# A third context buffer and regrouped tap operands, reordered small loads, and up-projection weights made one stage earlier

## The chip, the cores and the metric

The kernel runs on one core of one Trainium2 chip. The metric is the device time of one launch in microseconds (us), taken as the median of three runs. Below, PE is TensorE, DVE is VectorE, ACT is ScalarE, POOL is GpSimd, and SP is SyncE, which here only issues DMAs.

## The reference, cut to what matters

One decoder layer in fp32, batch 4, 1024 positions, width 512. Three sublayers, each followed by a layer norm: windowed self-attention, a cross-attention block with an S4D convolution and its own feed-forward part, and a second feed-forward part made of butterfly matrices. The parts that the change touches:

```python
K = 2.0 * jnp.einsum('dn,dnl->dl', dC, powers).real   # taps, (512, 1024)
K_ = (x_vision @ Wk)                                   # context keys, 4 x 2048 rows of 384
...
y = jnp.fft.irfft(xf * Kf.T[None], n=n, axis=1)[:, :L]
xt = x_text + y * (1 + gate * scale_out) + gate * shift_out
h = layernorm(xt, g_ffn, b_ffn)
h = gelu(h @ W1 + b1) @ W2 + b2                        # W1 (512, 2048)
xt = layernorm(xt + h, g_norm_out, b_norm_out)
...
h = butterfly(x @ W_exp + b_exp, up_weights, 2048)     # folded into w3, b3 by the kernel
h = butterfly(gelu(h + up_bias), down_weights, 2048)   # folded into w4
```

## The kernel before, in words

The kernel is a row of stages, each with its own on-chip buffers and semaphores. Between two stages all engines meet: DMAs have landed, POOL clears the semaphores of the stage, and then the next stage starts on every engine. So time saved or lost in a stage counts in full, and what the trace shows as idle at the start of a stage is on the path. Inside a stage every engine has its own list of instructions in the order in which the code is written, with waits on semaphores. There is no scheduler.

**Taps stage** (`stage_taps`, buffers `tp_`, 0 to 298 us). First the attention weights are folded (PE, ACT, to 72 us). Then four rounds, one for each 128 channels `c`: `turn(c, 0)` transposes the first power table in 32 PE transposes that ACT copies out in 8 (line 400); `key_groups(c)` loads four blocks of 512 context rows (`context`, line 201, on SP), transposes them and projects them on the key weights; `turn(c, 1)` does with the second table what `turn(c, 0)` did; `taps(c)` multiplies the tables (line 264, 32 fp32 matmuls of 128x128, which the trace records as 64), and ACT copies each group of four out of PSUM in four pieces of 32x128 into `krow` (line 409). Meanwhile DVE computes the tables of the next round (`first_table`, `second_table`). SP waits for `krow`, stores it, reads it back turned as `kd`, and only then comes to the context loads of the next round. There are two context buffers. The copy of the second table writes single floats 128 bytes apart, since `tabT[1]` is stored channel by channel; the matmul at line 264 reads its moving operand in single floats 512 bytes apart.

**Folding stage** (`stage_butterfly`, `bf_`, 298 to 437 us). SP loads `low_up` (2 MB), the bias of the expansion as a column of single floats, and `col_up` (four loads, 4096 runs of 16 bytes in all); ACT at the same time loads 8 MB of weights in rows of 8 and 4 KB. DVE multiplies out the low butterfly steps from `low_up` into `e_up` (line 844). PE then needs `e_up`, the bias and `col_up` all together for its bias product (line 747), from which the rest of the stage follows. At the end the result `w3` is stored by SP (line 701) and the bias `b3` by ACT (line 819), again as single floats.

**Inverse stage** (`stage_idft`, `id_`, 2732 to 2965 us). Four batches of four tiles; a tile is 96 matmuls of 128x512 on PE, some 12 us, then ACT and DVE form sum and difference, PE reverses the difference with an exchange matrix, ACT copies it to `rev` (two buffers) and POOL stores both.

**Feed-forward stage** (`stage_mlps`, `m_`, 2965 us to the end). Sixteen groups of 512 positions, for each 16 chunks of hidden units: `up` (12 matmuls into `ps_h`), Gelu on ACT (line 3006), split into high and low part on DVE (line 3138) and POOL, `down` (12 matmuls into `ps_o`). Every fp32 product is made of three fp32r products of high and low parts (`mm3`, lines 80 to 82). Before the first group the stage loads W1 in four slabs, scales it with `g_ffn` into high and low part (`up_hi` on ACT, `up_lo` on DVE), and adds `b_ffn @ W1` to the bias: `bias_products(s)`, 16 matmuls of one column, which the trace records as 32 (line 2873). One of these blocks stands ahead of the first transposes and three inside the first group. All of this waits for seven small loads, four of which are columns of single floats:

```python
up_slab(0)
for t, v in ((bf, ...b_ffn), (gf, ...g_ffn), (b1[:, 0, :], ...b1), (b1[:, 1, :], b3)):
    sp.dma_start(t[:, :], column(v), ...).then_inc(s_c, 16)      # 2730
for t, v in ((b2, ...), (g_row, ...), (b_row, ...)):
    sp.dma_start(t[:, :], row(v)).then_inc(s_c, 16)              # 2732
...
pe.wait_ge(s_c, 16 * 7)
bias_products(0)
for q in range(Q):
    turn(0, 0, q)
up(0, 0, 0, 0)
bias_products(1)
```

The order of the first four tiles there is fixed by the code too: POOL does `modulate(q + 1)` before `power(q)`, and ACT issues the loads of tile 3 only after the copy `hi` of tile 0.

## Time and profile before

| | us |
|---|---|
| median of three runs (lowest, highest) | 4554.81 (4554.34, 4557.46) |
| the profiled execution's own time | 4548.83 |
| its span in the trace | 4547.2 |
| taps stage (from the timeline) | 0 to 297.8 |
| folding stage | 297.8 to 437.2 |
| inverse stage | 2732.1 to 2964.7 |
| feed-forward stage | 2964.7 to the end |
| mean granted clock of TensorE, share of full speed | 0.944 |

The busy share of PE over the whole span is 87%. This is an average: in the stages between 437 and 2732 us nothing is changed, and the four stages of the table each have stretches in which PE stands still. The timeline of one engine has a bracket behind a row with the idle time before it and what ended it; the windows view gives busy time, granted clock and DMA share of a stretch.

### The profile page before, as it was taken

The numbers are of one execution on the slowest core, as the hardware profiler recorded it, in microseconds if no ns is written. First come the engines' busy times: TensorE is split into PE (matmuls) and PEld (weight loads), VectorE is DVE, ScalarE is ACT, GpSimd is POOL, SyncE is SP. The second block draws the span as 40 slices with busy tenths as digits, with TensorE's granted clock in tenths as the row PEclk, the third lists the DMA queues.
The fourth block names the chain that finished last, engine by engine and source line by source line (L and its number), as shares of the span: only waits on it lengthen the run. The fifth ranks groups of instructions, "written<-read, shape, count | busy, mean of one in ns | idle before, by whom it ended". The sixth has DMA issues, their size and how long they took to land. (4 is left out here: it accounts for less than half of the span.)

```text
span 4547.2 us, 61734 instructions
## 1 busy us (share of the span) xinstructions
PE 3933.9 (87%) x20188; PEld 3234.0 (71%) x20188; DVE 2528.2 (56%) x8674; ACT 1507.1 (33%) x2415; POOL 2027.3 (45%) x1411
## 2 busy tenths in 40 slices
PE   7856999958668888887899997959999999999998
PEld 4642778747668777786787775748877877778786
DVE  8815676578888888884555553224433445222222
ACT  3644454346546666664101002211111112111111
POOL 0000111157567787776564240036766765323332
PEclk9978999969889999998999998969999999999999
DMA  3454423220100111000542223341212232000000
GB/s 104 135 165 110 130 86 106 86 71 12 50 25 12 50 33 50 29 12 21 210 142 102 97 103 141 116 146 59 70 59 66 71 96 67 19 22 28 23 23 19
DMA packets 244938, 337.06 MB, mean 74 GB/s; under 512 B 66898, under 2 KB 125170, under 8 KB 241268
## 3 DMA queue, kind: packets, MB, share of 16 engines
q1 hardware_dynamic: 154868, 186.17, 13.5%
q10 hardware_dynamic: 87184, 138.46, 8.9%
q0 software_dynamic: 2560, 8.39, 0.5%
q8 instruction: 167, 2.74, 0.2%
q14 instruction: 159, 1.30, 0.1%
HBM read 220.70 MB, written 112.25 MB: 73 GB/s over the span
## 5 line engine op out<-in xcount | busy, mean ns | idle before, releaser
L2832 POOL TENSOR_TENSOR m_act_hl<-m_g,m_act_hl 128x512 fp32r<-128x512 f32 x256 | 355.3, 1388 | 681.0 <-DVE m_act_hl L3138 680.9
L1624 PE MATMUL xa_ps_t<-xa_diag,xa_s_buf 128*128 128x128 f32 x4096 | 520.6, 288 | 141.8 <-ACT xa_a L1711 74.8
L1624 PEld LDWEIGHTS xa_ps_t<-xa_diag,xa_s_buf 128*128 128x128 f32 x4096 | 507.7, 202 | 163.3 <-issue 81.0
L3138 DVE CAST m_act_hl<-m_g 128x512 fp32r<-128x512 f32 x256 | 139.6, 545 | 852.1 <-ACT m_g L3006 851.8
L1788 DVE MAX8 xa_cand<-xa_s_buf 128x8 f32<-128x64 f32 x4096 | 542.5, 218 | 63.3 <-ACT xa_s_buf L1674 37.4
L3006 ACT ACTIVATE m_g<-m_ps_h,m_b 128x512 f32<-128x512 f32 x256 | 176.1, 688 | 1117.7 <-PE m_ps_h L82 1112.6
L80 PE MATMUL m_ps_h<-m_hT,m_w 128*128 128x512 f32 x1024 | 417.7, 408 | 19.8 <-issue 17.7
L82 PE MATMUL m_ps_h<-m_hT,m_w 128*128 128x512 f32 x1024 | 409.8, 400 | 0.0
L81 PE MATMUL m_ps_h<-m_hT,m_w 128*128 128x512 f32 x1024 | 409.7, 400 | 0.0
L80 PE MATMUL m_ps_o<-m_w,m_act_hl 128*128 128x512 f32 x1024 | 407.1, 398 | 0.7 <-POOL m_act_hl L2832 0.7
L82 PE MATMUL m_ps_o<-m_w,m_act_hl 128*128 128x512 f32 x1024 | 406.9, 397 | 0.0
L81 PE MATMUL m_ps_o<-m_w,m_act_hl 128*128 128x512 f32 x1024 | 406.9, 397 | 0.0
L1552 POOL TENSOR_SCALAR xa_s_buf<-xa_s_buf,xa_top 128x1024 f32<-128x1024 f32 x120 | 342.9, 2858 | 141.4 <-ACT xa_prob L1693 141.4
L1554 POOL TENSOR_TENSOR xa_s_buf<-xa_s_buf,xa_prob 128x1024 f32<-128x1024 f32 x120 | 318.3, 2652 | 18.0 <-issue 0.4
L1674 ACT ACTIVATE xa_s_buf<-xa_ps_s 128x2048 f32<-128x2048 f32 x128 | 239.4, 1870 | 140.5 <-PE xa_ps_t L1624 75.4
L1693 ACT ACTIVATE xa_prob<-xa_s_buf,xa_nmax 128x2048 f32<-128x2048 f32 x128 | 252.6, 1998 | 88.0 <-POOL xa_s_buf L1554 88.0
L1591 PE MATMUL xa_ps_s<-xa_ks,xa_qs 128*128 128x512 f32 x512 | 159.2, 435 | 123.2 <-ACT xa_s_buf L1674 108.6
L80 PEld LDWEIGHTS m_ps_h<-m_hT,m_w 128*128 128x128 f32 x1024 | 195.7, 191 | 69.9 <-issue 24.8
L82 PEld LDWEIGHTS m_ps_h<-m_hT,m_w 128*128 128x128 f32 x1024 | 195.7, 191 | 47.4
L80 PEld LDWEIGHTS m_ps_o<-m_w,m_act_hl 128*128 128x128 f32 x1024 | 193.5, 189 | 48.7 <-POOL m_act_hl L2832 2.0
L81 PEld LDWEIGHTS m_ps_h<-m_hT,m_w 128*128 128x128 f32 x1024 | 196.4, 192 | 43.8
L82 PEld LDWEIGHTS m_ps_o<-m_w,m_act_hl 128*128 128x128 f32 x1024 | 193.8, 189 | 46.9
(384 smaller groups left out, 8329.6 us busy)
## 6 DMA issues: line engine op xcount, KB each, us to landing
at_xk<-in_x_dram SPq DMA_DIRECT2D x128, 128.0 KB, 2.8
spectrum<-df_yo ACTq DMA_DIRECT2D x32, 512.0 KB, 2.8
id_raw<-spectrum SPq DMA_DIRECT2D x32, 512.0 KB, 5.6
m_xt<-x ACTq DMA_DIRECT2D x64, 256.0 KB, 3.8
tp_awT<-in_ctx_dram SPq DMA_DIRECT2D x16, 768.0 KB, 4.6
xa_ks<-kt SPq DMA_DIRECT2D x48, 256.0 KB
xa_raw<-in_ctx_dram SPq DMA_DIRECT2D x32, 384.0 KB, 3.4
kt<-tp_aw SPq DMA_DIRECT2D x4, 2048.0 KB, 6.6
```

The costliest lines, as they stand in the source:

```text
L80: pe.matmul(out, w_hi, m_lo, start=start, stop=False)
L81: pe.matmul(out, w_lo, m_hi, start=False, stop=False)
L82: return pe.matmul(out, w_hi, m_hi, start=False, stop=stop)
L1552: pool.tensor_scalar(half, half, top[:, t % 2, h, TOPK - 1:TOPK], None, ALU.is_ge)
L1554: pool.tensor_tensor(half, half, prob[:, h % 2, HALF:S2], ALU.mult).then_inc(s_psel, 1)
L1591: last = pe.matmul(ps_s[:, c, :], qs[:, t % 2, h, :], ks[:, h, c * 512:(c + 1) * 512], start=True, stop=True)
L1624: last = pe.matmul(ps_t[:, c // 4, c % 4, :], s_buf[:, t % 2, h, k0:k0 + P], diag[:, h, :], start=(h == 0 and c % 4 == 0), stop=(h == HEAD ...
L1674: act.activation(s_buf[:, t % 2, h, :], ps_s[:, :, :].rearrange("p c n -> p (c n)"), ACT.Copy).then_inc(s_sc, 1)
L1693: act.activation(prob[:, h % 2, :], s_buf[:, t % 2, h, :], ACT.Exp, bias=nmax[:, t % 2, h:h + 1], scale=SCALE).then_inc(s_exp, 1)
L1788: dve.max(out=ranks[h][:, :, g], in_=s_buf[:, t % 2, h, :].rearrange("p (n g e) -> p g n e", g=SEGS, e=4)[:, g, :, :])
L2832: pool.tensor_tensor(lo, g32[:, :], hi.bitcast(F32), ALU.subtract).then_inc(s_gl, 1)
L3006: act.activation(g32[:, :], ps_h[:, n % 2, :], ACT.Gelu, bias=b1[:, cur, n:n + 1]).then_inc(s_g, 1)
```

## The change

Taps: a third context buffer (in a part of `aw` that the folding results use until they are stored, so SP waits for these stores before it loads the third block), context loads one block further ahead; the matmul at line 264 takes its columns in the order (r, d), so that it reads runs of four floats; `ps_k` has that order too; the copy of the second table writes runs of four floats and reads PSUM with a stride of 512 bytes; the copies to `krow` read PSUM with a stride of 16 bytes.

Folding: the bias and `col_up` are loaded ahead of `low_up`; biases come as ready [128, 16] tables, which the host lays out; `b3` is stored by rows, ahead of the `out_t` copies.

Inverse and feed-forward stage: W1's buffers become shared by both (`UpTiles`). The four slabs and the small columns (as ready tables) are loaded during batches 0 and 1; in batch 2 each tile is followed by one bias block on PE, four scalings on ACT and five instructions on DVE. `rev` has one buffer in place of two, and its copy waits until both stores of the tile before have landed. The inverse stage has eight semaphores more, the feed-forward stage two fewer.

```diff
@@ stage_taps @@
-        ps_k = psum("ps_k", [P, 2, 4, 4, R])
+        ps_k = psum("ps_k", [P, 2, 4, R, 4])
+        third = aw[:, 0, :, :].rearrange("p e n -> p (e n)")
+        raw = [... for r in (turned[:, 0:4 * DV], turned[:, 4 * DV:2 * 4 * DV], third[:, 0:4 * DV])]
...
-                    if g >= 2:
-                        sp.wait_ge(s_ct, VC * (g - 1))
+                    if g >= 3:
+                        sp.wait_ge(s_ct, VC * (g - 2))
...
                 context(1)
+                sp.wait_ge(s_fs[0], 16 * (DC + 2))
+                sp.wait_ge(s_fs[1], 16 * (DC + 1))
+                context(2)
...
-                                             tabT[0][:, :, d].rearrange("p r d -> p d r"), start=True, stop=True)
+                                             tabT[0][:, :, d], start=True, stop=True)
...
+                            out = tabT[1][...].rearrange("p (d r) -> p d r", r=R)
+                            act.activation(out[:, :, 4 * g:4 * g + 4], ps_t[:, n % 2, :, :].rearrange("p q d -> p d q"), ACT.Copy)
...
+                        products = ps_k[:, g % 2].rearrange("p q a d -> p q d a")
-                            last = act.activation(channels[:, :, d, :], ps_k[R * d:R * (d + 1), g % 2, :, d, :], ACT.Copy)
+                            last = act.activation(channels[:, :, d, :], products[R * d:R * (d + 1), :, d, :], ACT.Copy)
@@ stage_butterfly @@
-                sp.dma_start(low_up[:, 0:LOW_LEN], A["butterfly_up"]).then_inc(s_lu, 16)
-                sp.dma_start(wT[:, :, D:D + 1], A["L0_ffn_b_exp"].rearrange(...), allow_slow_non_contiguous=True)
+                sp.dma_start(bias[:, :], A["L0_ffn_b_exp_columns"]).then_inc(s_cup, 16)
                 for k in range(TOP):
                     sp.dma_start(col_up[:, k, :, :], ...).then_inc(s_cup, 16)
+                sp.dma_start(low_up[:, 0:LOW_LEN], A["butterfly_up"]).then_inc(s_lu, 16)
...
+                act.wait_ge(s_hi, 1)
+                act.dma_start(b3_out, upb[:, :]).then_inc(s_b3, 16)
                 for n in range(0, 16, 2):
...
-                act.dma_start(b3_out.rearrange("(c p) -> p c", p=P), upb[:, :], allow_slow_non_contiguous=True)
@@ stage_idft @@
-        rev = sb("rev", [P, 2, D])
+        rev = sb("rev", [P, D])
...
+                        if b == UPB:          # PE, after reverse(n - 1); UPB = 2
+                            bias_products(t)
...
+                def bias_products(s):
+                    pe.wait_ge(s_w1[s], 16)
...
+                    for n in range(4 * s, 4 * s + 4):
+                        for c in range(DC):
+                            last = pe.matmul(ps_b[:, n:n + 1], upt.raw1[:, c, n * P:(n + 1) * P], upt.bf[:, c:c + 1], ...)
...
-                    act.wait_ge(s_st[k], 32 * stores)
+                    if n >= 1:
+                        act.wait_ge(s_st[1 - k], 32 * ((n - 1) // 2 + 1))
@@ stage_mlps @@
-                up_slab(0)
-                for t, v in ((bf, ...), (gf, ...), (b1[:, 0, :], ...), (b1[:, 1, :], b3)):
-                    sp.dma_start(t[:, :], column(v), allow_slow_non_contiguous=True).then_inc(s_c, 16)
...
                 sp.wait_ge(s_mod, 2)
-                up_slab(1)
-                sp.wait_ge(s_mod, 3)
-                up_slab(2)
-                up_slab(3)
...
-                pe.wait_ge(s_c, 16 * 7)
-                bias_products(0)
```

The SP list of the folding stage, before:

```order
L686 DMA bf_low_up<-in_butterfly_up_dram 128x4064
L687 DMA bf_wT<-in_L_ffn_b_exp_dram 128x16x1
L689 DMA bf_col_up<-in_L_ffn_up_weights_dram 128x8x4 x4
L690 DMA bf_wv<-in_L_xattn_Wv_dram 128x3x512
L691 DMA bf_gate<-in_L_xattn_mod_gate_dram 128x1
```

and after:

```order
L694 DMA bf_bias<-in_L_ffn_b_exp_columns_dram 128x16
L696 DMA bf_col_up<-in_L_ffn_up_weights_dram 128x8x4 x4
L697 DMA bf_low_up<-in_butterfly_up_dram 128x4064
L698 DMA bf_wv<-in_L_xattn_Wv_dram 128x3x512
L699 DMA bf_gate<-in_L_xattn_mod_gate_dram 128x1
```

The 2 MB of `low_up` now stand behind the small pieces on the same queue.

The PE list where the inverse stage ends (`id_`) and the feed-forward stage (`m_`) begins, before:

```order
L2484 MATMUL id_ps_rev<-id_out,id_flip 128x512 x2
L2443 UNCONDITIONAL_BRANCH
L2853 UNCONDITIONAL_BRANCH
L2873 MATMUL m_ps_o<-m_bf,m_raw_33048 128x1 x16
L2861 MATMUL m_ps_t<-m_ident,m_h 128x128 x16
L80 MATMUL m_ps_h<-m_hT,m_w 128x512
```

and after:

```order
L2521 MATMUL id_ps_rev<-id_out,id_flip 128x512 x2
L2473 UNCONDITIONAL_BRANCH
L2902 UNCONDITIONAL_BRANCH
L2910 MATMUL m_ps_t<-m_ident,m_h 128x128 x16
L80 MATMUL m_ps_h<-m_hT,up_w 128x512
```

The block of 16 one-column matmuls is gone there. It now stands, four times, in batch 2 of the inverse stage, each time between the reversal and the next tile:

```order
L82 MATMUL id_ps<-id_y,id_mats 128x512
L2521 MATMUL id_ps_rev<-id_out,id_flip 128x512
L2555 MATMUL id_ps_b<-up_bf,up_raw_31619 128x1 x16
L80 MATMUL id_ps<-id_y,id_mats 128x512
L81 MATMUL id_ps<-id_y,id_mats 128x512
```

The four blocks, one ahead of the first transposes and three inside the first group, have moved between the tiles of batch 2.

## Rows read from the trace of the kernel before

**Rows 1.** The page: busy time and share of the span of each engine.

```profile
PE 3933.9 (87%) x20188; PEld 3234.0 (71%) x20188; DVE 2528.2 (56%) x8674; ACT 1507.1 (33%) x2415; POOL 2027.3 (45%) x1411
```

**Rows 2.** Groups by line and shape, whole span: busy, mean ns | idle before.

```profile
L1104 PE MATMUL at_ps_t<-at_xT,at_m_qk 128*128 128x128 f32 x1024 | 126.6, 278 | 2.4 <-ACTq L1187 2.4
...
L264 PE MATMUL tp_ps_k<-tp_tabT 128*128 128x128 f32 x256 | 57.0, 397 | 4.5 <-ACT tp_tabT L400 4.5
...
L409 ACT ACTIVATE tp_krow<-tp_ps_k 32x128 f32<-32x128 f32 x128 | 34.4, 269 | 27.4 <-PE tp_ps_k L264 26.3
```

**Rows 3.** The tile `tabT`: shortest, median and longest ns of its copies.

```profile
L400 ACT ACTIVATE tp_tabT<-tp_ps_t x64: 591/816/1147, 72.0 to 262.7; 128x512 f32<-128x512 f32 x64
```

**Rows 4.** Timeline of ACT, last round: start, duration, what, idle before.

```profile
256.33 7.36 ACT L400 ACTIVATE tp_tabT<-tp_ps_t 128x512 f32<-128x512 f32 x8
...
278.03 1.11 ACT L409 ACTIVATE tp_krow<-tp_ps_k 32x128 f32<-32x128 f32 x4 [0.64 <-PE tp_ps_k L264]
```

**Rows 5.** Timeline of PE: round 1 begins; last of three context waits.

```profile
123.03 1.06 PE L253 MATMUL tp_ps_t<-tp_ident,tp_tab 128*128 128x128 f32 x8
...
241.64 1.09 PE L282 MATMUL tp_ps_w<-tp_ident,tp_awT 128*128 128x128 f32 x8 [1.45 <-DMA tp_awT<-in_ctx_dram]
```

**Rows 6.** Timeline of DVE: the instruction behind the first table of round 1.

```profile
118.83 2.29 DVE L535 TENSOR_TENSOR tp_aw<-tp_aw 128x2048 fp32r<-128x2048 f32 x1 [0.17 <-issue]
```

**Rows 7.** DMA queues, 312 to 316 us: packets, MB, share of 16 engines.

```profile
q10 hardware_dynamic: 280, 1.56, 96.0%
q1 hardware_dynamic: 281, 0.00, 4.2%
```

**Rows 8.** DMA queues, 325 to 326 us.

```profile
q1 hardware_dynamic: 1508, 0.02, 85.1%
```

**Rows 9.** Timeline, folding stage: `low_up` is there, `e_up` ends, the bias product.

```profile
308.22 0.29 DVE L844 TENSOR_TENSOR bf_half<-bf_low_up 128x32 f32<-128x32 f32 x2 [49.45 <-DMA bf_low_up<-in_butterfly_up_dram]
...
311.81 2.36 DVE L844 TENSOR_TENSOR bf_e_up<-bf_half,bf_low_up 128x1024 f32<-128x1024 f32 x2
...
329.59 6.96 PE L747 MATMUL bf_ps_b<-bf_wT,bf_e_up 128*128 128x1 f32 x32 [9.25 <-issue]
```

**Rows 10.** Timeline: first instruction of the stage after folding.

```profile
437.23 0.20 POOL L1035 MEMSET at_ident<- 128x128 f32 x1 [138.78 <-POOLq L66]
```

**Rows 11.** Tile `b` (the store of `b3`): issue to landing.

```profile
DMA to landing us min/median/max: 14.3/14.3/14.3
```

**Rows 12.** Tile `bf_out_t` (16 stores of `w3`): issue to landing.

```profile
DMA to landing us min/median/max: 2.4/2.9/13.5
```

**Rows 13.** Timeline, end of the inverse stage and start of the next.

```profile
2956.81 0.54 POOL L2474 DMA_DIRECT2D conv<-id_rev  x1 [0.64 <-ACT id_rev L2524]
2964.65 0.37 SPq L2719 DMA_DIRECT2D m_raw<-in_L_xattn_W_dram  x1
```

**Rows 14.** The chain that ended last, feed-forward stage: start, us, what.

```profile
2981.55 13.75 issue
...
3000.83 6.20 issue
3007.03 1.30 POOLq L2795
...
3018.11 0.80 PE m_ps_h L80
```

**Rows 15.** Timeline of PE, first group: the second of four bias blocks.

```profile
3022.93 4.24 PE L2873 MATMUL m_ps_t<-m_bf,m_raw 128*128 128x1 f32 x32
```

**Rows 16.** Timeline of ACT: first and fifth Gelu of the first group.

```profile
3023.13 0.69 ACT L3006 ACTIVATE m_g<-m_ps_h,m_b 128x512 f32<-128x512 f32 x1 [4.50 <-PE m_ps_h L82]
...
3061.22 0.69 ACT L3006 ACTIVATE m_g<-m_ps_h,m_b 128x512 f32<-128x512 f32 x1 [3.16 <-PE m_ps_h L82]
```

**Rows 17.** Windows: PE, PEld, DVE, ACT, POOL busy; granted clock; DMA share; GB/s.

```profile
3027.20:3032.30 5.10, 5.10 (x13) 3.95 (x14) 2.10 (x4) 0.00 (x0) 0.00 (x0) 0.50 0.00 0
...
2809.00:2857.00 48.00, 47.04 (x197) 36.41 (x196) 15.78 (x18) 13.79 (x18) 4.32 (x8) 1.00 0.35 127
```

205 lines of the change are left out of this document (96 added, 109 removed).

## The prediction

> **What bounds the kernel now.** I read the page first. TensorE is busy for 87% of the span [rows 1], but that is a mean over stages, and the stages meet at barriers, so I went stage by stage: the timelines of the engines in the four stages that change, the chain of waits at the start of the feed-forward stage, the DMA queues where loads compete, and the windows for the clock. The reader is to see four things. In the taps stage PE and ACT take turns on the path: a strided copy of tables lasts 7.4 us for eight [rows 4], a plain one is half as long [rows 3], and ACT waits 26 us for the tap matmuls [rows 2]. In the folding stage PE waits until 329.6 us for small loads, though `e_up` was ready at 311.81 + 2.36 = 314.2 [rows 9]. In the inverse stage PE is busy 47.0 of 48 us at full clock [rows 17]: whatever is added to PE there is paid. At the start of the feed-forward stage PE does nothing useful from 2964.65 to 3018.11 us [rows 13, 14].
>
> All sums are against the profiled execution (4548.8 us, of it 4547.2 span). The median of the runs shown is 6 us higher; I take the same distance for the new kernel and subtract from 4554.8.
>
> **Taps.** *Matmuls at line 264.* 256 records are busy for 57.0 us, 0.223 each; the like matmul with contiguous operands takes 126.6 / 1024 = 0.124 [rows 2]. No row shows a read in runs of four; its bounds are these two. I take the fast end. Then a group of 8 records takes 1.0 us on PE, and the four copies to `krow` (1.11 us [rows 4]) set the pace. Before, a group took 1.11 + 0.64 = 1.75 us. *Copies to `krow`* now read PSUM 16 bytes apart. Nothing in the trace reads PSUM with a stride. Upper bound: what a stride costs on the write side, (1147 - 591) / 512 = 1.09 ns an element [rows 3], so 4 x 128 x 1.09 ns = 0.56 us a group, and the pace is 1.67; lower bound nothing. *Copies of the second table* now write four floats in a row, but read PSUM at 512 bytes: between 591 ns, where PE's transposes set the pace (5.0 us for eight), and 7.4 us as now; a loss if both sides were to cost is at most another 0.5 us for each of the eight. I take the cheap end for both, as the engine that now pays a stride pays it in SBUF. A round then gives 8 x (1.75 - 1.15) = 4.9 and 7.4 - 5.0 = 2.4, together 7.3 us.
>
> *Third buffer.* It removes three waits of PE for a context block (the last is 1.45 us [rows 5], the others 2.4 and 0.6): 4.4 us. The new wait of SP for the folding stores stands ahead of a load that is needed 10 us later, and only context loads are queued behind it: nothing.
>
> *What is late next.* Round 1 starts on PE at 123.03 [rows 5], but its table is ready only at 118.8 [rows 6]. So round 0 can give only 4.2 us. In the later rounds DVE has two tables of some 18 us and 2.3 us for the keys [rows 6], 39 us for a round of 44. Sum: 4.2 + 3 x 7.3 + 4.4 = **30.5 us**; with both stride bounds against it, 4 x 8 x 0.08 + 4.4, about 7, and below nothing only if the table copies got slower as well.
>
> The Trainium skill (SBUF: State Buffer, the note on cachelines in "Door 1: The DMA port swizzle") says that SBUF is fetched in lines of 16 bytes and that several accesses to one line run at full rate. Four fp32 fill such a line; with it the fast end for line 264 would hold. The trace agrees as far as it goes: floats 128 bytes apart cost 1147 against 591 ns.
>
> **Folding.** *Start.* The two queues give packets in turn: 280 against 281 while both are full [rows 7]; alone, small ones go at 1508 a microsecond [rows 8]. ACT's queue has 8.39 MB in 1536 packets. Put first, the 128 bias packets and 4096 pieces of `col_up` get one turn each beside them, so 1536 are through when the bulk ends. The bulk loses the competition of `low_up` (2.08 MB at 0.4 MB/us = 5.2 us) and ends at 325.4 - 5.2 = 320.2. The other 2688 take about 2.3 us at the mean of 325 to 329 us (1190 a us), to 322.5; only then comes `low_up`, 5.1 us, landed at 328.1. `e_up` takes 314.2 - 308.2 = 6.0 us from its arrival [rows 9], so the bias product starts at 334.2 in place of 329.6 [rows 9]: **4.6 us lost**. What was the early load becomes the late one.
>
> *End.* The store of `b3` lands 14.3 us after its issue at 418.8, and the last stores of `w3` need up to 13.5 instead of 2.9 us [rows 11, 12], as its 2048 pieces alternate with them. Stored by rows it is 128 packets, issued 12 us earlier. The last `w3` store (issued at 420.6) then lands 13.5 - 2.9 = 10.6 us sooner, and the next stage (437.2 [rows 10]) with it; 0.3 us goes to the issue ahead of the first copy. Net for the stage: 10.3 - 4.6 = **5.7 us gained**, bounds -2 (only half of the end) and +16 (the start gains after all).
>
> **Inverse stage.** Four bias blocks go on a PE that never waits. One lasts 4.24 us [rows 15], the two after it 3.8 and 4.0: 4 x 4.0 = 16. Then the clock: behind each block in the first group the granted clock is at half (1.2 GHz) though large matmuls run, 5.1 us after the second [rows 17], about 3 and 6 after the others. PE had run at nearly full clock before the block, and the block itself is one-column matmuls. Half of that time is lost: some 2.3 us a block, 9 in all. Bounds: 0 and 24 (half clock for the whole 12 us tile). ACT's four scalings (0.7 us each) and DVE's five instructions lie beside 12 us of matmuls; the copies for batch 3 wait for their own loads longer than that. The loads come during batch 1, whose DMA share is 0.35 [rows 17].
>
> `rev` with one buffer costs at the end: the copy of tile 15 now waits until the store of tile 14, issued at 2955.0, has landed (2.3 us and more), where before its own store went out at 2956.8 [rows 13]: 2.0 us, 1 to 4.5. Eight more semaphores to clear: 0.7. Sum: **27.7 us lost**.
>
> **Feed-forward stage.** *Until the first `up`.* The chain has 13.75 us behind `modulate(1)`, in which PE, ACT and DVE wait for the seven small loads and then do the first block and scaling, and 6.20 us for tile 3 [rows 14], whose loads ACT issues only behind the copy of tile 0. Without the block, `power(0)` runs at 2981.6, normalisation, transposes and copy of tile 0 end at 2985, so tile 3's loads are issued at 2984.4 instead of 2999.0. They share the queues with 3 MB of W2, which SP now issues at 2981.6: 2 MB at 0.39 MB/us and 2 us of latency put tile 3 at 2992, not 3007.03. From there to the first `up` it is 3018.11 - 3007.03 = 11.1 us as before [rows 14], so 3003: **15 us gained** (12 to 17).
>
> *First group.* From first to fifth Gelu 38.1 us pass [rows 16]. Without the three blocks it is 2.8 + 3 x 5.7 = 19.9 (24 matmuls at 47.04 / 197 = 0.239 us are 5.7 [rows 17]): **18.2 us gained**, of it 12.0 the blocks themselves and the rest mostly clock. Two semaphores fewer: 0.2.
>
> **Sum.** 30.5 + 5.7 - 27.7 + 33.4 = 41.9 gained; I hold back 2 for reads in runs of four that come out a little above the contiguous ones: 40. The time is 4554.8 - 40 = **4515 us**.
>
> **Rivals.**
> (A) *Strided PSUM reads cost what strided SBUF writes cost.* The table copies stay at 7.4 us and the `krow` copies set a pace of 1.67. For it: the path of an operand is one float wide on both sides. Against: the only stride seen is on a write. Taps then give 7, the total is 4554.8 - (7 + 5.7 - 27.7 + 33.4) = 4536. The Trainium skill (PSUM: Partial Sum Buffer, "Specifications (TRN2)") gives PSUM lines of 8 bytes and says that a non-contiguous access there slows matmuls significantly; by that rule this rival is what happens. No row here reads PSUM so.
> (B) *The early small loads do help.* If small pieces on an engine's ring were not held to one turn each, they would be through at 303, `low_up` at 309, and the product could start when the transposes are done, about 316: 13 gained in place of 4.6 lost, total 4497. Against it stand 280 and 281 packets.
> (C) *Slower.* The bias blocks break the clock in the inverse stage for the whole of batch 2. It decides once a block is followed by half clock for more than a tile (12 us): four tiles of 96 matmuls then take 23 in place of 11.5 us, 46 lost beside the 16. The total, with the taps of (A), is 4554.8 - (7 + 5.7 - 65 + 33.4) = 4574. Against it: after the blocks in the first group the clock came back within 6 us each time.
> (D) *The third buffer and the regrouping do nothing*, since DVE's tables set the rounds: excluded beyond round 0 by 39 against 44 us.
>
> **How the numbers follow.** Forecast 0.55, (A) 0.22, between the two 0.08, (B) 0.08, (C) 0.05, rest 0.02. The likeliest case alone spans 4506 to 4525. The range reaches to (A): 4503 to 4538. Changes under 0.2% (9 us) can't be told from none; faster 0.92, same 0.04, slower 0.04, the last two from (C) and from (A) with the bad ends of the inverse and the folding stage.
>
> **What will show it.** Right: line 264 near 0.13 us a record and `krow` copies back to back; `tabT` copies all near 0.6 us; the bias product at about 4.6 us later within its stage than before, waiting for DVE; the `w3` stores landing in 3 us at the end; four blocks of 4 us in batch 2 with a clock of 0.5 in the windows behind them; the first `up` 38 us after its stage's start (53 before). Wrong: table copies over 0.9 us (A), `low_up` landing before 320 us of the old time (B), tiles of batch 2 over 20 us (C).

## The result and the profile after

The changed kernel takes 4512.6 us (median of 4 runs, 4508.6 to 4517.8), the kernel before beside it 4554.9 (4554.3 to 4557.5): ratio 0.9907, 95% interval 0.989 to 0.9924. A second series on another chip gave 0.9914 (0.9901 to 0.9927), 4513.2 against 4553.6. Forecast were 4515 us and a range of 4503 to 4538. Faster by 0.9%, as the likeliest case had it.

The profiled executions differ by less than the medians: 4548.8 and 4517.8 us. So I took a second trace of each kernel and compared the stages one by one. Each length runs from the first instruction of a stage to that of the next.

| stage | before, two traces | after, two traces | difference, pair by pair | forecast |
|---|---|---|---|---|
| taps (from 0) | 297.8, 300.4 | 270.3, 269.1 | -27.4, -31.3 | -30.5 |
| folding | 139.5, 139.2 | 135.2, 135.4 | -4.3, -3.8 | -5.7 |
| attention | 481.9, 482.3 | 482.7, 482.6 | 0.8, 0.2 | 0 |
| cross-attention | 1234.2, 1241.3 | 1243.8, 1237.7 | 9.6, -3.6 | 0 |
| film and transform | 578.8, 578.9 | 578.8, 578.6 | 0, -0.2 | 0 |
| inverse | 232.5, 232.6 | 255.7, 255.4 | 23.2, 22.8 | 27.7 |
| feed-forward | 1582.6, 1582.6 | 1549.7, 1549.6 | -32.8, -32.9 | -33.4 |

The four changed stages give 41.4 us in the first pair and 45.3 in the second; the medians say 42.3 and 40.4. What made the first pair of traces differ by only 31.0 is the cross-attention stage, 9.6 us longer though nothing in it was changed. The windows over this stage, first before and then after (columns as in [rows 17]):

```profile
919.10:2153.30 1234.20, 949.89 (x6528) 892.68 (x6528) 1035.10 (x5795) 732.61 (x992) 896.57 (x410) 0.93 0.11 32
```

```profile
888.20:2132.00 1243.80, 958.38 (x6528) 901.42 (x6528) 1034.29 (x5795) 732.66 (x992) 897.21 (x410) 0.91 0.11 32
```

DVE, ACT and POOL are as busy as before; PE is 8.5 us busier at a granted clock of 0.91 in place of 0.93. This comes and goes within one kernel (second traces: 1241.3 before, 1237.7 after) and says nothing on the change.

**Taps.** Groups by line, the answer to [rows 2], and the tile with both power tables, the answer to [rows 3] (shortest, median, longest ns):

```profile
L269 PE MATMUL tp_ps_k<-tp_tabT 128*128 128x128 f32 x256 | 35.7, 286 | 4.7 <-ACT tp_tabT L405 2.7 <-ACT tp_krow L416 1.4
L416 ACT ACTIVATE tp_krow<-tp_ps_k 32x128 f32<-32x128 f32 x128 | 34.5, 269 | 8.0 <-PE tp_ps_k L269 5.2
```

```profile
L402 ACT ACTIVATE tp_tabT<-tp_ps_t x32: 591/597/606, 71.5 to 214.2; 128x512 f32<-128x512 f32 x32
L405 ACT ACTIVATE tp_tabT<-tp_ps_t x32: 594/597/617, 101.3 to 240.5; 128x512 f32<-128x512 f32 x32
```

The tap matmuls fell from 57.0 to 35.7 us. The copies to `krow` now read PSUM 16 bytes apart and last 269 ns, to the nanosecond what they lasted; the copies of the second table (L405) read it 512 bytes apart and last 597, like those of the first, which read it in a row. The next two fences are the timelines of ACT and of PE: the round's 32 `krow` copies stand back to back and then ACT and PE wait for DVE's first table of round 1, as the prediction had it; and of the three context waits in rounds 1 to 3 one is left (another, in round 0, was there before too).

```profile
107.71 9.33 ACT L416 ACTIVATE tp_krow<-tp_ps_k 32x128 f32<-32x128 f32 x32 [1.25 <-PE tp_ps_k L269]
118.97 0.60 ACT L402 ACTIVATE tp_tabT<-tp_ps_t 128x512 f32<-128x512 f32 x1 [1.93 <-PE tp_ps_t L258]
```

```profile
118.28 1.09 PE L258 MATMUL tp_ps_t<-tp_ident,tp_tab 128*128 128x128 f32 x8 [2.38 <-DVEq L529]
...
136.79 1.36 PE L287 MATMUL tp_ps_w<-tp_ident,tp_awT 128*128 128x128 f32 x8 [2.13 <-DMA tp_awT<-in_ctx_dram]
```

**Folding.** The queues while the small pieces and the bulk of ACT's queue compete (285 to 290 us, as [rows 7]), and the timeline around the bias product (as [rows 9]):

```profile
q10 hardware_dynamic: 488, 1.93, 98.8%
q1 hardware_dynamic: 489, 0.01, 6.0%
```

```profile
302.02 0.29 DVE L852 TENSOR_TENSOR bf_half<-bf_low_up 128x32 f32<-128x32 f32 x2 [63.63 <-DMA bf_low_up<-in_butterfly_up_dram]
...
308.19 6.96 PE L755 MATMUL bf_ps_b<-bf_bias,bf_e_up 128*128 128x1 f32 x32 [20.20 <-DVEq L855]
...
405.49 0.21 POOL L1043 MEMSET at_ident<- 128x128 f32 x1 [134.48 <-POOLq L66]
```

Packet for packet again, 488 against 489. The stage starts at 270.3, so the product starts 37.9 us into it and not 31.8: 6.0 us lost, and PE now waits for DVE, whose input is what came late. At the end `b3` lands 1.4 us after its issue [rows 11: 14.3] and no `w3` store needs more than 3.0 [rows 12: 13.5]: 10.3 gained.

**Inverse stage.** PE behind the second bias block, and the windows of the block before it and of the 2 us behind this one:

```profile
2865.84 1.70 PE L2555 MATMUL id_ps_b<-up_bf,up_raw 128*128 128x1 f32 x14
2867.40 0.48 PE L80 MATMUL id_ps<-id_y,id_mats 128*128 128x512 f32 x1
...
2868.20 0.63 PE L80 MATMUL id_ps<-id_y,id_mats 128*128 128x512 f32 x1
```

```profile
2846.00:2850.00 4.00, 4.00 (x35) 3.70 (x33) 1.28 (x2) 3.04 (x5) 1.08 (x2) 1.00 0.17 68
2868.00:2870.00 2.00, 2.00 (x7) 1.57 (x6) 2.00 (x4) 0.00 (x0) 0.00 (x0) 0.53 0.00 0
```

During the block the granted clock is still 1.00; it is at half (1.2 GHz) behind it, in the first microseconds of the next tile, and comes back. The blocks start at 2846.5, 2863.9, 2881.3 and 2898.8, one every 17.4 us, where tiles came every 12.3 (kernel before, same batch): 5.2 us a block, 3.5 the block and 1.7 the clock. Four of them are the 20.8 us by which the last matmul of the last tile ends later (241.0 us into the stage for 220.2). The end of the stage (as [rows 13]):

```profile
2956.85 0.60 ACT L2576 ACTIVATE id_rev<-id_ps_rev 128x512 f32<-128x512 f32 x1 [3.05 <-DMA conv<-id_rev]
2958.10 0.54 POOL L2511 DMA_DIRECT2D conv<-id_rev  x1 [2.43 <-ACT id_rev L2576]
2966.47 0.35 SPq L2785 DMA_DIRECT2D m_b<-in_L_xattn_b_dram  x1
```

**Feed-forward stage.** The chain at its start (as [rows 14]) and the first and fifth Gelu (as [rows 16]):

```profile
2967.20 9.50 issue
...
2990.74 8.80 issue
2999.54 1.30 POOLq L2844
...
3010.62 0.80 PE m_ps_h L80
```

```profile
3015.65 0.69 ACT L3023 ACTIVATE m_g<-m_ps_h,up_b 128x512 f32<-128x512 f32 x1 [4.51 <-PE m_ps_h L82]
...
3035.36 0.69 ACT L3023 ACTIVATE m_g<-m_ps_h,up_b 128x512 f32<-128x512 f32 x1 [4.38 <-PE m_ps_h L82]
```

The wait of 13.75 us is gone. The other one, for tile 3, has grown from 6.20 to 8.80, and the first `up` comes 44.2 us after the stage's start: 9.3 us sooner than before, not 15 (11.2 in the second pair of traces: 43.4 for 54.6). From first to fifth Gelu it is 19.7 us, 18.4 less.

### The profile page after: what moved, and what is told of

Read it like the earlier page. It is cut to its first block and busy times, and to the rows that moved or that the text cites. A ratio compares the mean times of both kernels' runs of the same rounds, so it can differ in the third digit from the quotient of the medians.

```text
span 4516.2 us, 61725 instructions
## 1 busy us (share of the span) xinstructions
PE 3909.1 (87%) x20188; PEld 3212.3 (71%) x20188; DVE 2526.9 (56%) x8674; ACT 1494.5 (33%) x2415; POOL 2029.2 (45%) x1411
## 5 line engine op out<-in xcount | busy, mean ns | idle before, releaser
L1632 PE MATMUL xa_ps_t<-xa_diag,xa_s_buf 128*128 128x128 f32 x4096 | 532.1, 291 | 142.9 <-ACT xa_a L1719 74.8
L1632 PEld LDWEIGHTS xa_ps_t<-xa_diag,xa_s_buf 128*128 128x128 f32 x4096 | 518.9, 206 | 164.5 <-issue 81.1
L3023 ACT ACTIVATE m_g<-m_ps_h,up_b 128x512 f32<-128x512 f32 x256 | 176.1, 688 | 1101.4 <-PE m_ps_h L82 1096.3
L80 PE MATMUL m_ps_h<-m_hT,up_w 128*128 128x512 f32 x1024 | 413.7, 404 | 19.6 <-issue 17.6
L81 PE MATMUL m_ps_h<-m_hT,up_w 128*128 128x512 f32 x1024 | 408.6, 399 | 0.0
L82 PE MATMUL m_ps_h<-m_hT,up_w 128*128 128x512 f32 x1024 | 407.5, 398 | 0.0
L80 PE MATMUL m_ps_o<-m_w,m_act_hl 128*128 128x512 f32 x1024 | 405.6, 396 | 0.7 <-POOL m_act_hl L2881 0.7
L80 PEld LDWEIGHTS m_ps_h<-m_hT,up_w 128*128 128x128 f32 x1024 | 194.5, 190 | 70.1 <-issue 24.5
L1549 POOL TENSOR_TENSOR xa_aT<-xa_a,xa_aT 128x512 fp32r<-128x512 f32 x128 | 162.1, 1287 | 150.9 <-ACT xa_a L1719 150.9
L80 PEld LDWEIGHTS m_ps_o<-m_w,m_act_hl 128*128 128x128 f32 x1024 | 192.8, 188 | 48.9 <-POOL m_act_hl L2881 2.1
L82 PEld LDWEIGHTS m_ps_h<-m_hT,up_w 128*128 128x128 f32 x1024 | 194.3, 190 | 45.6
```

Source lines behind the costliest of these rows:

```text
L80: pe.matmul(out, w_hi, m_lo, start=start, stop=False)
L81: pe.matmul(out, w_lo, m_hi, start=False, stop=False)
L82: return pe.matmul(out, w_hi, m_hi, start=False, stop=stop)
L1549: pool.tensor_tensor(aT[:, 1, 4 * g:4 * g + 4, :], a32[:, g % 2, :, :], aT[:, 0, 4 * g:4 * g + 4, :].bitcast(F32), ALU.subtract).then_inc( ...
L1632: last = pe.matmul(ps_t[:, c // 4, c % 4, :], s_buf[:, t % 2, h, k0:k0 + P], diag[:, h, :], start=(h == 0 and c % 4 == 0), stop=(h == HEAD ...
L3023: act.activation(g32[:, :], ps_h[:, n % 2, :], ACT.Gelu, bias=b1[:, cur, n:n + 1]).then_inc(s_g, 1)
```

## The experiments

Unless said otherwise each kernel is the changed one with one edit. Times are medians with the ratio to the kernel before and its 95% interval; stage lengths come from each kernel's trace and are the sharper measure, since the cross-attention stage adds some 10 us of its own to and fro. The traces of runs 5 and 6 differ from the others in one more thing, ahead of the edit and on code that no edit here touches: the film and transform stage lasts 574.1 to 574.2 us in place of 578.8 (577.9 in run 1), and the second tile of the inverse stage starts 35.5 us after the stage's start in place of 37.8. The windows from 30 to 40 us after that start, for the changed kernel and for run 6, differ in the granted clock:

```profile
2740.80:2750.80 10.00, 9.92 (x34) 7.67 (x35) 4.45 (x5) 0.60 (x1) 0.00 (x0) 0.78 0.00 0
```

```profile
2733.00:2743.00 10.00, 9.92 (x44) 7.87 (x43) 4.30 (x5) 0.60 (x1) 0.79 (x1) 1.00 0.05 18
```

No run tells why. In runs 5 and 6 some 2.2 us are therefore to be added to the inverse stage before it is compared.

**1. The strided read of the moving operand (taps).**

```diff
-ps_k = psum("ps_k", [P, 2, 4, R, 4])
+ps_k = psum("ps_k", [P, 2, 4, 4, R])
-                 tabT[0][:, :, d], start=True, stop=True)
+                 tabT[0][:, :, d].rearrange("p r d -> p d r"), start=True, stop=True)
```

The copies to `krow` read `ps_k` without a stride again, too.

> The changed kernel with one edit in the taps stage: ps_k and the moving operand of the tap matmuls (line 269) have the order of the kernel before again, single floats 512 bytes apart; the copies to krow read PSUM without a stride again. Theory (the strided read of the moving operand made these matmuls slow, the strided PSUM reads of ACT cost nothing): a record takes 0.22 us in place of 0.14, the krow copies wait 0.64 us for each group again and last 0.27 us as now, each of the last three rounds is 5 us longer and the first up to 4: taps 284 to 289 us in place of 269. Rival 1 (strided PSUM reads cost ACT something that the faster matmuls pay for): krow copies under 0.27 us, and the stage at most 10 us longer. Rival 2 (DVE's tables set the rounds): no change.

4529.2 us, 0.9949 (0.9934 to 0.9964). Taps end at 286.8, 16.5 later. The groups by line:

```profile
L269 PE MATMUL tp_ps_k<-tp_tabT 128*128 128x128 f32 x256 | 57.0, 397 | 2.7 <-ACT tp_tabT L405 2.7
L415 ACT ACTIVATE tp_krow<-tp_ps_k 32x128 f32<-32x128 f32 x128 | 34.5, 270 | 27.3 <-PE tp_ps_k L269 26.1
```

The theory holds: single floats 512 bytes apart in SBUF cost PE 21.3 us over 256 records, and the ACT copy is 270 ns with a plain read of PSUM, 269 with a strided one.

**2. The copy of the second table (taps).**

```diff
-out = tabT[1][...].rearrange("p (d r) -> p d r", r=R)
-act.activation(out[:, :, 4 * g:4 * g + 4], ps_t[:, n % 2, :, :].rearrange("p q d -> p d q"), ACT.Copy)
+out = tabT[1][...].rearrange("p (d r) -> p r d", r=R)
+act.activation(out[:, 4 * g:4 * g + 4, :], ps_t[:, n % 2, :, :], ACT.Copy)
```

> The changed kernel with one edit in the taps stage: the copy of the second table writes single floats 128 bytes apart again and reads PSUM without a stride. Theory (the write side alone has the cost): these copies take 1.15 us again in place of 0.6, eight of them 7.4 to 9.2 in place of 5; the rounds are 2.4 to 4 us longer, taps 277 to 283 in place of 269. Rival 1 (PE's transposes and the context work set the pace while ACT copies): copies of 1.15 us but a stage of 269 to 271. Rival 2 (the read stride was what is cheap only by chance of four-float runs): copies under 1.0 us.

4522.0 us, 0.9932 (0.9915 to 0.9949); taps end at 279.1, 8.7 later, some 2.2 a round. Same tile, same columns as above:

```profile
L405 ACT ACTIVATE tp_tabT<-tp_ps_t x32: 1023/1078/1152, 103.4 to 247.8; 128x512 f32<-128x512 f32 x32
```

The write side alone carries the cost.

**3. The third buffer (taps).**

```diff
-                sp.wait_ge(s_fs[0], 16 * (DC + 2))
-                sp.wait_ge(s_fs[1], 16 * (DC + 1))
-                context(2)
-                        if g + 3 < KB * DC:
-                            context(g + 3)
+                        if g + 2 < KB * DC:
+                            context(g + 2)
```

> The changed kernel with two context buffers in place of three, and SP's order and waits as before. Theory (the third buffer is worth the three waits of PE for a context block, 4.4 us in the kernel before, and somewhat more now that the rounds are shorter while the loads are not): taps 273 to 278 us in place of 269, with PE or ACT waiting for DMA tp_awT at the start of rounds 1 to 3. Rival (the waits are not on the path; ACT's work sets the pace): taps within 1 us of 269.

4521.6 us, 0.9931 (0.9915 to 0.9946); taps end at 278.4, 8.0 later than in the first trace of the changed kernel (nine traces with its taps stage end it between 268.7 and 270.7). The waits of PE for a context block (us in total, times, longest), first before the change, then with two buffers, then with three:

```profile
PE tp_ps_w L282 <- DMA tp_awT<-in_ctx_dram: 6.1, 4, 2.4
```

```profile
PE tp_ps_w L284 <- DMA tp_awT<-in_ctx_dram: 13.0, 5, 6.6
```

```profile
PE tp_ps_w L287 <- DMA tp_awT<-in_ctx_dram: 4.3, 2, 2.2
```

With shorter rounds the loads that did not get shorter are missed by more: 13.0 where it had been 6.1. So the third buffer is worth 8 us in the new rounds. What it removes against the kernel before these waits don't settle, as they vary from trace to trace. The second traces, before and after, have

```profile
PE tp_ps_w L282 <- DMA tp_awT<-in_ctx_dram: 7.7, 4, 2.1
```

```profile
PE tp_ps_w L287 <- DMA tp_awT<-in_ctx_dram: 3.3, 2, 1.8
```

1.8 us less waiting in the first pair, 4.4 in the second, for the 4.4 of my sum.

**4. `low_up` first (folding).**

```diff
+sp.dma_start(low_up[:, 0:LOW_LEN], A["butterfly_up"]).then_inc(s_lu, 16)
 sp.dma_start(bias[:, :], A["L0_ffn_b_exp_columns"]).then_inc(s_cup, 16)
 ...
-sp.dma_start(low_up[:, 0:LOW_LEN], A["butterfly_up"]).then_inc(s_lu, 16)
```

> The changed kernel with one edit: in the folding stage low_up is loaded ahead of the bias table and of col_up, as in the kernel before; the bias stays a ready table. Theory (small pieces and the bulk of the other queue take turns on each DMA engine, so the small ones must stand last): low_up lands about 10.5 us after the stage's start and not 31.7; the bias product starts 30 to 32 us after the start and not 37.9, at the low end because 2048 single floats of bias have become 128 rows. The stage lasts 127.5 to 129.5 us in place of 135.2, the kernel 6 to 7.7 us less than the changed one, about 4506. Rival 1 (the 8 MB of the other queue set the time, whatever stands where): the product still starts at 37 to 38, nothing gained. Rival 2 (late col_up is what hurts, the small ones first was right): col_up lands at 40 us or later and the stage gets longer by 2 us or more.

4505.5 us, 0.989 (0.9875 to 0.9905). The stage lasts 128.6 us in place of 135.2. The bias product starts 30.3 us after the stage's start (268.7):

```profile
299.01 6.96 PE L755 MATMUL bf_ps_b<-bf_bias,bf_e_up 128*128 128x1 f32 x32 [7.59 <-issue]
```

So the new load order costs 6.6 us, and the bias as a table alone gains 1.5 against [rows 9] (30.3 for 31.8).

**5. The bias blocks in one piece (inverse).** All 64 matmuls stand behind the second tile of batch 2; DVE's scalings follow behind this tile and the next two:

```diff
-                        if b == UPB:
-                            bias_products(t)
+                        if b == UPB and t == 1:
+                            bias_products()      # all slabs
```

> The changed kernel with all four bias blocks of the inverse stage in one piece of 64 matmuls behind the second tile of batch 2; the scalings on DVE follow in the gaps of this and the two next tiles. Theory (the clock falls once for each piece, and comes back after 4 us of large matmuls): the piece takes 14 us, half clock follows once, 1.9 us lost in place of 7.4; the inverse stage lasts 250 us in place of 255.7, the kernel takes 5.5 us less than the changed one, about 4507. Rival 1 (the loss grows with the time spent on one-column matmuls): half clock for 12 us or more behind it, or inside the piece, the stage as long as now or longer. Rival 2 (the clock has nothing to do with the blocks): half clock at places that don't follow the blocks.

4520.3 us, 0.9925 (0.9911 to 0.9938); the inverse stage lasts 260.0 us, 4.3 more and not 5.5 less, and 6.5 more once the 2.2 us of this trace are added. The timeline of PE, and windows across the piece:

```profile
2849.23 25.36 PE L2553 MATMUL id_ps_b<-up_bf,up_raw 128*128 128x1 f32 x128
```

```profile
2850.00:2856.00 6.00, 6.00 (x36) 6.00 (x35) 0.04 (x1) 2.47 (x5) 1.08 (x2) 0.61 0.23 87
2856.00:2862.00 6.00, 6.00 (x30) 6.00 (x29) 0.00 (x0) 0.00 (x0) 0.00 (x0) 0.50 0.00 0
...
2880.00:2882.00 2.00, 2.00 (x11) 1.64 (x10) 0.00 (x0) 0.00 (x0) 0.00 (x0) 1.00 0.00 0
```

My theory fell; rival 1 holds. In one piece the clock falls inside the piece, which then runs on at half (25.4 us in place of 4 x 3.5 = 14.0), and stays at half some 4 us beyond it. In four pieces each block had ended before the clock fell. The small blocks between tiles were the cheaper form.

**6. The bias blocks where PE waits anyway.** The blocks and the low parts of W1 go from batch 2 to the start of the feed-forward stage; the loads and the high parts stay.

```diff
-                        if b == UPB:             # inverse stage, PE; the same on DVE with up_lo(t)
-                            bias_products(t)
+                for n in range(HC):              # feed-forward stage, PE, ahead of the first transposes
+                    for c in range(DC):
+                        last = pe.matmul(ps_o[:, 0, n:n + 1], raw1[:, c, n * P:(n + 1) * P], upt.bf[:, c:c + 1], ...)
```

> The changed kernel with the four bias blocks and the low parts of W1 (DVE) taken out of batch 2 of the inverse stage and put at the start of the feed-forward stage, where PE stands still for 22 us; W1's loads and the high parts (ACT) stay in the inverse stage. The last four low parts come in the first group. Theory (the blocks cost 3.5 us each plus 1.85 us of half clock on a PE that never waits, and nothing on a PE that waits for its first tiles): a tile of batch 2 takes 12.1 us and not 17.4, the inverse stage 234.5 us in place of 255.7; the blocks are done 17 us after the next stage's start; the first up stays at 44 us (plus 0 to 1); the kernel takes 20 to 21 us less than the changed one, about 4492. Rival 1 (DVE's twelve low parts stand ahead of tile 0 and hold it, and with it the loads of tile 3): first up at 46 to 48, gain 17 to 19. Rival 2 (the blocks slow the clock of the first group more than they do now): 4500 or more.

4497.0 us, 0.9878 (0.9863 to 0.9893). The inverse stage lasts 232.5 us, as before the change, though it still carries W1's loads, the high parts on ACT and the single `rev`. Part of that is this trace's early start: with its 2.2 us added the stage is 234.7, the 234.5 that I expected, so of the 23.2 us lost there some 21 are the blocks and the clock behind them, and some 2 are `rev` and the semaphores. The feed-forward stage is 4.5 us longer (1554.2), since at half clock the blocks take twice as long:

```profile
2935.59 27.44 PE L2922 MATMUL m_ps_o<-up_bf,up_raw 128*128 128x1 f32 x128 [11.34 <-PEq L66]
2964.18 1.09 PE L2883 MATMUL m_ps_t<-m_ident,m_h 128*128 128x128 f32 x4 [1.15 <-DVE m_h L3052]
```

27.4 us, where I had put 17 from the warm blocks; the first `up` comes at 46.4. DVE, start of the third four low parts, of tile 0's statistics, and of the bias addition:

```profile
2956.24 2.74 DVE L3105 SCALAR_TENSOR_TENSOR up_w<-up_raw,up_gf,up_w 128x512 fp32r<-128x512 f32 x4 [0.94 <-PE m_ps_o L2922]
2958.89 0.69 DVE L3036 BATCH_NORM_STATS2 m_stats<-m_xt 128x6 f32<-128x512 f32 x1
...
2963.06 0.17 DVE L3113 TENSOR_TENSOR up_b<-up_b,m_ps_o 128x16 f32<-128x16 f32 x1 [2.38 <-PE m_ps_o L2922]
```

Rival 1 holds: the twelve low parts end 23.4 us after the stage's start and hold tile 0, which POOL had finished at 14.2, and with it tile 3's loads. The slow blocks are what makes them late, since each four wait for their block, and the bias addition, which stands ahead of tile 0's normalisation, waits for the last block until 27.5. First `up` at 46.4 is what the rival said; the gain, 16 us by the medians, is a little less than its 17 to 19.

**7. W2 held back (feed-forward).**

```diff
-                sp.wait_ge(s_mod, 2)
+                sp.wait_ge(s_mod, 3)
                 for s in range(1, SLABS):
                     down_slab(s)
```

> The changed kernel with one edit: SP issues the last three slabs of W2 (3 MB) after the third modulate of the first group, not after the second. Theory (tile 3's four loads, issued 22.5 us after the stage's start, take 10.6 us to land because they share the DMA engines with W2): tile 3 lands 28 to 30 us after the start in place of 33.1, the first up comes at 39 to 41 in place of 44.1, the kernel takes 3 to 5 us less than the changed one, about 4508.5. Rival (the loads of tile 3 are slow by themselves, or POOL's modulate and power set the pace): first up still at 44, nothing gained; if W2 then comes too late for the first down matmuls, the first group gets longer by 1 us or more.

4511.1 us, 0.9905 (0.9889 to 0.992); by time alone not to be told from the changed kernel. By the trace the stage is 6.6 us shorter (1543.1). POOL's `modulate` of tile 3, and the first `up` (the stage starts at 2967.66):

```profile
2994.12 1.27 POOL L2843 TENSOR_TENSOR m_xt<-m_xt 128x512 f32<-128x512 f32 x1 [2.04 <-DMA m_xt<-x]
```

```profile
3005.17 0.79 PE L80 MATMUL m_ps_h<-m_hT,up_w 128*128 128x512 f32 x1 [1.41 <-DVE m_hT L3078]
```

Tile 3 is there 26.5 us after the start in place of 33.1, the first `up` 37.5 after it: the 38 that I had forecast without this edit. W2's 3 MB beside tile 3 are the missing 6 us: its loads, issued at 21.2 here and 22.5 in the changed kernel, need 5.3 us in place of 10.6.

**8. The ready tables without the move.** The two last stages of the kernel before, with tables in place of columns of single floats (taps and folding as in the changed kernel; the diff is to the kernel before):

```diff
-sp.dma_start(t[:, :], column(v), allow_slow_non_contiguous=True).then_inc(s_c, 16)
+sp.dma_start(t[:, :], v).then_inc(s_c, 16)      # b_ffn, g_ffn, b1 as [128, n] tables, b3 stored by rows
```

> Taps and folding as in the changed kernel; inverse and feed-forward stage as in the kernel before, except that b_ffn, g_ffn, b1 and b3 come as ready tables of 16 or 4 floats a row. So the up weights are made in the feed-forward stage again. Theory (much of the time before the first up was the wait for 5120 single floats, and the tables alone remove it): the small loads are there 12 us after the stage's start and not 29, the first bias block runs until 19, tile 3's loads are issued at 22 to 23; they share the engines with 6 MB of W1 and W2, so the first up comes at 44 to 47 (53.5 before, 44.1 in the changed kernel). The first group takes 18.4 us more than in the changed kernel, the inverse stage 23.2 us less. Total within 5 us of the changed kernel, about 4512. Rival 1 (my forecast's account: the move itself is worth 6 us or more beyond the tables): first up at 50 or later, 4518 to 4524. Rival 2: nearly nothing of the start is due to single floats, 4522 and more.

4518.0 us, 0.9921 (0.9908 to 0.9935), 5.4 us above the changed kernel; between the theory and rival 1. The first bias block starts 13.9 us after the stage's start (19.6 in the first, 19.5 in the second trace of the kernel before):

```profile
2956.34 6.96 PE L2881 MATMUL m_ps_o<-m_bf,m_raw 128*128 128x1 f32 x32 [22.97 <-DMA m_b_row<-_L_xattn_b_norm_out_dram]
```

The first `up` comes after 48.0 us (53.5 before, 44.2 changed). By stages: inverse 232.5, feed-forward 1575.9. So of the 32.8 us gained in the feed-forward stage the tables alone give 6.7 and the move 26.2; the move costs 23.2 in the inverse stage. Its net worth is 3 us by the stages, 5 by the medians; the intervals of the two ratios overlap, so by time alone it is not shown.

**9. Both kernels again.**

> The changed kernel once more, beside the kernel before on the same chip. The stage of the cross-attention, which the change does not touch, lasted 1234 us in the one trace of the kernel before and 1243.8 in the one of the changed kernel. Theory (this stage has two lengths some 10 us apart, whatever the kernel, by the clock granted in it): over the timed runs the ratio is again 0.990 to 0.992, a gain of 38 to 45 us, as the sum of the changed stages says, and the profiled cross stage lasts either 1232 to 1235 or 1240 to 1245. Rival (the change makes the cross stage slower): 1240 to 1245 in this trace, and 1232 to 1235 in the next trace of the kernel before.

> The kernel before once more, for its profile. Theory: the cross stage takes 1240 to 1245 us here, or 1232 to 1235, by chance; with the former the execution takes 4553 to 4558. Rival (its length belongs to the kernel): 1232 to 1235 again, and 4547 to 4550 in all. The four changed stages last what they did, within 1 us: 296.8, 139.5, 232.5 and 1582.6.

0.9914 (0.9901 to 0.9927) for the changed kernel; the kernel before took 4558.9 in its one run. Their cross-attention stages lasted 1237.7 and 1241.3 us, so this one is neither of two fixed lengths, nor does it belong to the kernel. The changed stages repeat within 1.3 us, but for the taps of the kernel before (297.8 and 300.4).

**10. Versions made of the findings.** Both have 4 and 7, tile 3's loads ahead of the copy of tile 0, a free half of `a_sb` for the last reversed tile, and the blocks out of batch 2. In the first, one block stands behind the last reversal and three ahead of the first transposes. In it POOL still stores the last reversed tile from `rev`, so that those 128 rows of `conv` are another tile's.

```diff
-                hi(0, 0, 0)
                 load(0, 0, 3, 0)
+                hi(0, 0, 0)
 ...
+                    if n == B * TC - 1:
+                        act.activation(a_sb[:, 0, :], ps_rev[:, k, :], ACT.Copy).then_inc(s_rc, 1)
+                        return
```

> A version made of what the experiments showed. Against the changed kernel: low_up first; no bias block and no low part of W1 in batch 2; the first bias block stands behind the last reversal of the inverse stage, where PE otherwise only waits for the stores, the other three at the start of the feed-forward stage (3 x 6.9 us at half clock, done 21 us after the start); low parts of slabs 0 to 3 at the end of the inverse stage, ahead of tile 0, ahead of tile 2 and in the first group; tile 3's loads issued ahead of the copy of tile 0; the last three slabs of W2 after the third modulate; the last reversed tile is copied to a free half of a_sb, so that it need not wait for the store before it. Expected by stage: folding 128.6, inverse 231 to 232, first up 35.5 to 38 us after its stage's start (44.1), first group as now: 6.6 + 24 + 7 = 38 us less than the changed kernel, about 4475 (4468 to 4482). Rival 1 (the first transposes wait for the blocks, and the low parts on DVE delay tile 0, so that the gains at the start are lost): 4482 or more. Rival 2 (a bias block at the end delays the meeting of the engines): inverse stage 234 or more.

4482.9 us, 0.9841 (0.9827 to 0.9854): folding 128.1, inverse 234.0, first `up` after 38.2. Some 30 us less than the changed kernel, 8 short of what I expected. The inverse stage is at rival 2's threshold, 234; without the block behind the last reversal it lasts 232.7 (next version), so that block, with its four low parts on DVE, costs 1.3 us.

> The version made of what the experiments showed, with the bias blocks all in the feed-forward stage: three ahead of the first transposes (20.6 us at half clock), the fourth behind the transposes of tile 0; the low parts of slabs 0 and 1 ahead of tile 0 on DVE, of 2 and 3 in the first group; POOL does power(2) ahead of modulate(3); tile 3's loads ahead of the copy of tile 0, W2's last slabs after the third modulate; low_up first; the last reversed tile is stored from a free half of a_sb. Expected: folding 128.5, inverse 230.7 (232.5 with single rev buffer cost taken off), first up 34.5 to 36 us after its stage's start (44.1 in the changed kernel, 38.2 in the version before this one), first to fifth Gelu 19.7. Total 6.6 + 25 + 9 = 40 us less than the changed kernel: 4472 (4467 to 4480). Rival 1 (DVE's eight low parts per two chunks slow the first group): first to fifth Gelu 21 or more, 4476 or more. Rival 2 (the fourth block holds tile 1's transposes and with them the rest): first up still at 38, 4475.

4482.7 us, 0.9844 (0.9828 to 0.9859), beside the changed kernel's 0.9914 on the same chip: the best version, 71 us below the kernel before and 30.5 below the changed one. It is 10.7 us above what I had expected. Folding 127.5, inverse 232.7: I had expected 230.7, because I took run 6's 232.5, with its early start, for the length without blocks. The feed-forward stage lasts 1547.2, with the first `up` after 39.7 us (start at 2934.70). DVE's second four low parts, then PE:

```profile
2948.56 5.78 DVE L3119 SCALAR_TENSOR_TENSOR up_w<-up_raw,up_gf,up_w 128x512 fp32r<-128x512 f32 x4 [4.09 <-PE m_ps_o L2932]
```

```profile
2934.74 20.61 PE L2932 MATMUL m_ps_o<-up_bf,up_raw 128*128 128x1 f32 x96 [9.20 <-PEq L66]
2958.13 1.09 PE L2892 MATMUL m_ps_t<-m_ident,m_h 128*128 128x128 f32 x4 [2.78 <-DVE m_h L3066]
2959.01 6.83 PE L2932 MATMUL m_ps_o<-up_bf,up_raw 128*128 128x1 f32 x32
2965.70 1.09 PE L2892 MATMUL m_ps_t<-m_ident,m_h 128*128 128x128 f32 x4
2968.66 1.11 PE L2892 MATMUL m_ps_t<-m_ident,m_h 128*128 128x128 f32 x4 [1.87 <-DVE m_h L3066]
```

Rival 2's mechanism holds, with more lost than it said. DVE's eight low parts end 19.6 us after the start and hold tile 0 (transposes at 23.4); the fourth block then holds tile 1 until 31.0, and tiles 2 and 3 follow at once. The gap that this block was to fill was no longer there.

## Why the prediction was right, step by step

- **Tap matmuls, `krow` and table copies: right.** The fast end was chosen for each, 0.124 us a record on PE, nothing for PSUM strides; measured 35.7 / 256 = 0.139, 269 and 597 ns. Rounds 1 to 3 begin on PE at 118.3, 165.1 and 209.0 (before 123.0, 177.9, 228.8), and with the starts at 70.8 and 71.3 the four rounds gain 4.2, 8.1, 7.0 and 7.6: the first is held by DVE's table, as forecast. (8 x 0.6 is 4.8 and not the 4.9 of the sum; nothing hangs on it.) Rival (A) is refuted by runs 1 and 2 from both sides. The Trainium skill (PSUM: Partial Sum Buffer, "Specifications (TRN2)") says that non-contiguous PSUM access slows matmuls significantly; for ACT as the reader these two runs show no nanosecond of it, at strides of 16 and 512 bytes. For a matmul that writes PSUM so no run here has an answer. The Trainium skill's rule of 16-byte lines (SBUF: State Buffer, "Door 1: The DMA port swizzle") agrees with runs of four at 275 ns a record against 396 for single floats (medians).
- **Third buffer: right in kind, its size not settled.** I put 4.4 us for three waits removed. In the first pair of traces 1.8 us of PE's waiting went, and the wait of round 1 stayed (2.1 us); in the second pair it was 4.4. Run 3 says what I had not asked: in the new rounds the buffer is worth 8. The taps gave 27.4 and 31.3 us for 30.5.
- **Folding: right in both signs.** Start 4.6 lost forecast, 6.0 measured, since `low_up` was there 31.7 us into the stage and not 30.3; end 10.3 forecast and measured. The lower bound of -2 does not follow from half of the end, 10.3 / 2 - 4.6 = 0.5. The mechanism of the turns was shown by run 4: order restored, 6.6 us back. Rival (B) is refuted.
- **Inverse stage: right mechanism, 4.5 us too dear.** 5.2 us a block where I had 4.0 + 2.3; I had taken the block's length from the first group ([rows 15]: 4.24), between the 3.5 of a block at full clock and the 7.0 of one at half. My reading that PE had run at nearly full clock before each of those blocks was wrong: ahead of the third, which began where the window of [rows 17] ends, the clock was at half all the time, and only then did it rise (0.85 in the window 3032 to 3034, 1.00 in the 2 us behind).

```profile
3032.30 3.77 PE L2873 MATMUL m_ps_t<-m_bf,m_raw 128*128 128x1 f32 x32
```

In batch 2 PE does come from full clock, and the four blocks are alike. `rev`: the last store goes out 4.2 us after the last reversal starts, for 2.4 before, so 1.8 (2.0 forecast). From the last landing to the next stage it is 6.1 us for 5.5, so the semaphores cost some 0.6; no row stood behind my 0.7. Rival (C) is refuted: half clock for some 4 us behind a block, not 12.
- **First `up`: the step that failed.** "2 MB at 0.39 MB/us and 2 us of latency put tile 3 at 2992": I let tile 3 share the queues with 1 of the 3 MB of W2, and had its loads issued 19.8 us after the start where it was 22.5. Tile 3 came 33.1 us after the start, not 27.4. Run 7 shows W2 to be the cause: held back, it leaves tile 3 at 26.5.
- **First group: right**, 18.2 forecast, 18.4 measured.
- **Not foreseen:** from the fifth Gelu to the end the changed kernel is 4 to 5 us faster (1480.9 for 1486.0; second traces 1481.2 for 1485.2). It has W1 in buffers that stand elsewhere, and the `up` matmuls of L80 last 403 ns for 406. Without the move (run 8) it is 1485.3 and 405, so it comes with the move; why, no run here tells. This hid the miss at the first `up`: 9.3 + 18.4 + 5.1 = 32.8 for 33.4.

So the mechanisms were right but for the first `up`, and that the sum came so close, 41.9 forecast and 41.4 measured in the first pair of traces (45.3 in the second), was in part luck: misses of 3 to 6 us cancel. In that pair the taps gave 3.1 less than forecast and the first `up` 5.7 less, the inverse stage cost 4.5 less, and the `up` matmuls gave 5.1 that were not forecast at all.

## What to carry to other kernels

When rounds get shorter, count again the waits for what did not get shorter: a prefetch buffer is worth what it saves in the new rounds (8 us in run 3), and its gain is not the sum of the old waits (4.4). One-column matmuls placed on a PE that never waits cost 1.5 times their own length through the clock; moved into the start of a stage where the clock is at half they last twice as long, and the path pays only for what they hold up: 4.5 us in run 6, for some 21 in batch 2. Look again at how large the gap is after every other move. When an edit seems to bring a stage back to its old length, look whether the trace differs ahead of the edit too. Before moving work across stages, try the cheap half of the edit alone: here the ready tables gave 6.7 us without cost, the move another 3 net.

## What the runs showed of the hardware

- Where a piece of one-column matmuls is short (3.5 us), the granted clock is 1.00 during it and half for some 4 us of large matmuls behind it; where it is long (25.4 us), the clock is 0.50 through most of it and some 4 us beyond. A block of 32 records takes 3.5 us at full clock and 6.8 to 7.0 at half.
- ACT reads PSUM at a stride of 16 bytes (269 ns for 32x128) or 512 bytes (597 for 128x512) as fast as in a row (270 and 597); it writes SBUF in runs of four floats as fast as in a row (597 ns for 128x512), in single floats 128 bytes apart in 1078.
- Small and large packets of two queues on the same engines go by count, 488 against 489, while their bytes go 0.01 against 1.93 MB.
- The cross-attention stage, the same code in all kernels, lasted between 1231.9 us (run 1) and 1244.4 (run 8), with a granted clock of 0.93 in the short and 0.91 in the long one of the first two traces. The film and transform stage lasted 574.1 and 574.2 us in two traces (runs 6 and 5) and 577.9 to 578.9 in the others. What decides this stays open.
